# Gathered rows of the expert tiles moved inside SBUF on two DMA queues and transposed on VectorE, gates copied two tiles sooner

## The chip, the cores and the metric

The kernel runs on one core of one Trainium2 chip. The metric is the device time of one execution in microseconds (us); lower is better. The kernel before takes 640.49 us, the median of three runs (639.61 to 642.61).

A core has five engines with an instruction stream each, and they meet only through semaphores: TensorE (PE; its weight loads are listed as PEld), VectorE (DVE), ScalarE (ACT), GpSimd (POOL) and SyncE (SP), which here does nothing but issue DMAs. The 16 DMA engines of the core move the data. SBUF is the on-chip memory, PSUM the eight accumulator banks that TensorE writes.

## What is computed

The input is eight sequences of 512 tokens of width 256. After a layer norm, two branches are added to the residual: a causal linear attention with a second-order Taylor feature map (16 heads), and a mixture of eight experts in which each token goes to its top two.

```python
x  = L0_attn_hidden_states                      # (8, 512, 256) f32
xn = _layernorm(x)
x  = x + attention(xn, Wq, Wk, Wv, Wo) + experts(xn, Wg, W1, W2, W3)

# experts: E = 8, TOP_K = 2, DIM = 256, HID = 512
logits = xf @ Wg
top_w, top_i = top_k(logits, 2);  top_w = softmax(top_w)
h = einsum('nc,ech->enh', xf, W1)
g = einsum('nc,ech->enh', xf, W2)
y = einsum('enh,ehc->enc', silu(h) * g, W3)
out = einsum('enc,ne->nc', y, combine)          # combine holds top_w at the two experts
```

The kernel computes an expert only for the tokens that were sent to it: 8192 pairs of a token and an expert, sorted by expert in lists that are padded to whole tiles of 128 rows, 71 tiles in all (`NT`).

## The kernel before

**Attention first, experts after.** Up to about 300 us the kernel does the attention and the routing. On the way GpSimd scatters each normed token (256 values, 8 gates and its number) into a DRAM scratch, `xs_scr`, at its two places in the sorted lists. Then comes the loop over the 71 expert tiles, which this change is about.

**One expert tile t.** GpSimd gathers its 128 rows into a ring `xg` (`GR` = 4 slots, `gather`). TensorE transposes them in two halves into PSUM bank 4 (`transpose_g`, L1286). ScalarE copies the bank to `xgh` in a rounded format (L695), VectorE writes what the rounding left out to `xgl` (L1078), so that a product is made of three matmuls (high by high, high by low, low by high). Straight after that VectorE copies the gates and the row number from `xg` to a ring `xw` (L1083). TensorE computes h and g, six matmuls of 512 columns each (`up`, L1297). ScalarE applies silu to h (L722), VectorE multiplies by g into `hs` (L1112).

**The turn of s = silu(h) * g.** The second product needs s transposed. For tiles 8 to 68 (`TS` to `TE` - 1) this is not done by TensorE: SyncE issues four DMAs that regroup `hs` inside SBUF into `hq` (`move_h`, L450), two iterations later VectorE transposes `hq` in blocks of 32 x 32 into bank 5 (`turn_s`, L1088), ScalarE and VectorE split the bank into `sTh` (L706) and `sTl` (L1092), and TensorE runs the twelve matmuls of 256 columns (`down`, L1318) one iteration after. VectorE weighs the result with the gate (`weigh_y`, L1100) and GpSimd scatters it with an add into the output (`scatter`, L570).

**What sets the order.** Each engine's program is written out by hand as a loop over t; waits are semaphores counted. In iteration t from 11 on: TensorE does up(t, 0), up(t, 1), transpose_g(t+1), down(t-3). VectorE does the multiply of t, `xgl` and gates of t+1, turn_s(t-2), weigh_y(t-3), `sTl` of t-2. ScalarE does silu(t), `xgh` of t+1, `sTh` of t-2. SyncE does move_h(t), which waits for the multiply of t and, since `hq` has two slots, for turn_s(t-2). ScalarE's silu of t waits until move_h(t-2) has landed, since it writes into the slot of `hs` that this move reads. GpSimd issues gathers ahead of each scatter, up to t+7 ahead of scatter(t); a gather waits for the transposes and the copy of gates that last read its slot.

## Time and profile before

| | before |
|---|---|
| median of 3 runs | 640.49 us (639.61 to 642.61) |
| profiled execution, its own time | 641.93 us |
| profiled execution, span first to last instruction | 640.1 us |
| mean granted TensorE clock | 0.998 of full speed |
| PE busy in the span | 615.1 us (96%) |
| DVE, ACT, POOL busy | 450.3, 348.0, 360.3 us |
| bytes moved by DMA | 80.37 MB |

Busy time counts an engine's own instructions; issuing a DMA is not counted as busy. Matmuls overlap in the pipeline, so a matmul of 0.40 us can start 0.23 us after the one before it: what a matmul costs is the distance from start to start, not its duration. A wait is put down to whatever released it last. In the views by line, L numbers are lines of the kernel before.

### The profile page before, as it was taken

How to read it: one execution, taken by the hardware profiler on the slowest of the kernel's cores; microseconds unless marked ns; L12 is line 12 of the kernel's file. 1: busy time of each engine (PE TensorE's matmuls, PEld its weight loads, DVE VectorE, ACT ScalarE, POOL GpSimd, SP SyncE). 2: the span in 40 equal slices, each digit the busy share in tenths (PEclk: the TensorE clock that was granted, in tenths of full speed). 3: DMA queues.
4: the chain of work that ended last, by engine and by line, in shares of the span. 5: the costliest groups of instructions: out<-in, count | busy, mean ns of one | idle time of the engine just before them, and what ended most of it. 6: DMA issues, size and time to landing. Idle time of an engine off the chain costs nothing.

```text
span 640.1 us, 16670 instructions
## 1 busy us (share of the span) xinstructions
PE 615.1 (96%) x5181; PEld 475.5 (74%) x5181; DVE 450.3 (70%) x1134; ACT 348.0 (54%) x515; POOL 360.3 (56%) x453
## 2 busy tenths in 40 slices
PE   8899999999999999998899899999999999999995
PEld 8565665666666666655788788888888888888884
DVE  6876878787787776587787466666666667666663
ACT  3678878787878777775564233333333333333331
POOL 4265564737364654657167366566666666656645
PEclk9999999999999999999999999999999999999999
DMA  4753554545544444552953465656655656656553
GB/s 133 176 121 102 132 159 112 152 95 153 137 103 124 99 121 100 159 140 89 334 149 65 100 126 119 121 119 126 126 117 125 120 120 126 120 120 122 123 96 43
DMA packets 73347, 80.37 MB, mean 126 GB/s; under 512 B 12368, under 2 KB 61392, under 8 KB 73264
## 3 DMA queue, kind: packets, MB, share of 16 engines
q1 hardware_dynamic: 56144, 50.72, 30.1%
q0 software_dynamic: 16704, 28.12, 22.2%
q8 instruction: 48, 0.79, 0.5%
q10 hardware_dynamic: 416, 0.46, 0.3%
q14 instruction: 35, 0.29, 0.2%
HBM read 27.72 MB, written 22.95 MB: 79 GB/s over the span
## 4 chain that ended last, share of the span: by engine, by line
PE 43%; issue 26%; POOL 17%; DVE 8%; POOLq 2%; ACT 2%; DMA 0%; DVEq 0%; ACTq 0%
PE banks L1171 10%; POOL xg L544 9%; PE banks L1153 8%; PE banks L1191 7%; POOL out L570 6%; PE banks L1297 5%; PE banks L1200 4%; PE banks L1235 4%; POOL mark L556 3%; POOLq L554 2%; PE banks L1318 2%; PE banks L1220 2%; PE banks L1226 1%; ACT T L607 1%; DVE xTl L828 1%
## 5 line engine op out<-in xcount | busy, mean ns | idle before, releaser
L570 POOL DMA_INDIRECT out<-yo,xw x71 | 112.6, 1586 | 103.8 <-DVE yo L1100 99.9
L535 POOL TENSOR_SCALAR_AFFINE_SELECT T<-T 128x512 f32<-128x512 f32 x128 | 81.2, 646 | 108.6 <-ACT T L613 45.0
L1297 PE MATMUL banks<-w12h,xgh 128*128 x284 | 113.0, 398 | 3.4 <-DVE xgl L1078 3.3
L1297 PE MATMUL banks<-w12l,xgh 128*128 x284 | 111.4, 392 | 0.0
L1297 PE MATMUL banks<-w12h,xgl 128*128 x284 | 111.0, 391 | 0.0
L1112 DVE TENSOR_TENSOR hs<-banks,hs 128x512 f32<-128x512 f32 x71 | 49.1, 692 | 85.2 <-PE banks L1297 81.0
L706 ACT ACTIVATE sTh<-banks 128x512 fp32r<-128x512 f32 x71 | 42.4, 599 | 93.4 <-DVE banks L1088 76.8
L544 POOL DMA_INDIRECT xg<-xs_scr,glist x71 | 71.8, 1012 | 24.5 <-issue 19.7
L1171 PE MATMUL banks<-T,vau 128*17 128x512 f32 (+3 forms) x1024 | 75.5, 434 | 0.3 <-POOL T L535 0.3
L526 POOL DMA_INDIRECT xs_scr<-xb,slots x64 | 63.6, 994 | 19.0 <-issue 12.5
L1153 PE MATMUL banks<-Q,K 32*128 32x256 f32 (+2 forms) x1024 | 70.0, 358 | 2.0 <-DMA K<-Kt 1.8
L722 ACT ACTIVATE hs<-banks 128x512 f32<-128x512 f32 x71 | 42.4, 598 | 46.2 <-DMA hq<-hs 16.3
L599 ACT ACTIVATE T<-banks 128x1024 f32<-128x1024 f32 x64 | 62.1, 1027 | 10.0 <-PE banks L1153 9.4
L607 ACT ACTIVATE T<-banks 128x768 f32<-128x768 f32 x64 | 48.5, 810 | 29.1 <-PE banks L1153 26.4
L1297 PEld LDWEIGHTS banks<-w12h,xgh 128*128 128x128 f32 x284 | 53.6, 189 | 13.7 <-issue 4.8
L1297 PEld LDWEIGHTS banks<-w12h,xgl 128*128 128x128 f32 x284 | 53.3, 188 | 11.8
L695 ACT ACTIVATE xgh<-banks 128x256 fp32r<-128x256 f32 x71 | 27.3, 385 | 62.1 <-PE banks L1286 44.5
L1171 PEld LDWEIGHTS banks<-T,vau 128*17 128x17 f32 x1024 | 26.1, 97 | 45.5 <-issue 39.2
L1297 PEld LDWEIGHTS banks<-w12l,xgh 128*128 128x128 f32 x284 | 53.6, 189 | 8.1
L613 ACT ACTIVATE T<-banks 128x768 f32<-128x768 f32 x64 | 48.6, 809 | 19.0 <-PE banks L1153 18.5
L1092 DVE TENSOR_TENSOR sTl<-banks,sTh 128x512 fp32r<-128x512 f32 x71 | 48.9, 690 | 13.9 <-ACT sTh L706 11.1
L1153 PEld LDWEIGHTS banks<-Q,K 32*128 32x128 f32 x1024 | 38.4, 183 | 25.1 <-ACT T L599 10.9
(186 smaller groups left out, 1245.6 us busy)
## 6 DMA issues: line engine op xcount, KB each, us to landing
hq<-hs SPq DMA_DIRECT2D x244, 64.0 KB
w12r<-w SPq DMA_DIRECT2D x16, 512.0 KB, 4.4
Q<-Q SPq DMA_DIRECT2D x126, 64.0 KB, 2.4
out<-xa SPq DMA_DIRECT2D x16, 256.0 KB
w3r<-w SPq DMA_DIRECT2D x8, 512.0 KB, 7.1
K<-Kt SPq DMA_DIRECT2D x126, 32.0 KB
xa<-x SPq DMA_DIRECT2D x7, 512.0 KB, 4.8
xg<-xs_scr,glist POOLq DMA_INDIRECT x71
```

Source lines behind the costliest of these rows:

```text
L526: e.indirect_dma_start(xs_d, bass.IndirectOffsetOnAxis(slots[:, k, 4 * b + blk:4 * b + blk + 1].bitcast(U32), 0), xb[b % 2][:, blk, :], No ...
L535: e.affine_select(out=v, in_=v, pattern=[[0, 4], [1, P]], compare_op=ALU.is_ge, fill=-1.0, base=0, channel_multiplier=-1).then_inc(s["g_mk ...
L544: e.indirect_dma_start(xg[:, t % GR, :], None, xs_d, bass.IndirectOffsetOnAxis(glist[:, t:t + 1].bitcast(U32), 0)).then_inc(s[f"d_g{t % GR ...
L570: e.indirect_dma_start(out, bass.IndirectOffsetOnAxis(xw[:, t % XR, NE:NE + 1].bitcast(U32), 0), yo[:, t % 2, :], None, compute_op=ALU.add ...
L599: e.activation(T0[n % 2][:, 2 * h:2 * h + 2, :], banks[:, 2 * h:2 * h + 2, :], ACT.Square, scale=0.25, bias=1.0).then_inc(s["a_s"], 1)
L607: e.activation(T1[:, 2 * h:2 * h + 2, :], banks[:, 2 * h:2 * h + 2, 0:384], ACT.Square, scale=0.25, bias=1.0).then_inc(s["a_s"], 1)
L613: e.activation(T2[:, 2 * h:2 * h + 2, :], banks[:, 2 * h:2 * h + 2, P:512], ACT.Square, scale=0.25, bias=1.0).then_inc(s["a_s"], 1)
L1092: e.tensor_tensor(s_turned(sTl, t), s_bank(t), s_turned(sTh, t).bitcast(F32), ALU.subtract).then_inc(s["v_st"], 1)
L1112: e.tensor_tensor(h_turned(t), h_bank(t, 1), h_turned(t), ALU.mult).then_inc(s["v_mu"], 1)
L1153: i = e.matmul(banks[:, r, c0:c0 + w], K2[rr, g, h, jm * P:(jm + 1) * P], Q2[g][rr, h, p, 512 - w:512], start=(p == 0), stop=(p == 1))
L1171: i = e.matmul(banks[32 * r:32 * r + HA, 4, 512 - w:512], vau[b % 2][:, jm, 4 * qd + r, :], v[:, r, :], start=(jm == 0), stop=(jm == 2), s ...
L1297: i = e.matmul(banks[:, 2 * (t % 2) + m, :], a[:, k, :], w[:, bass.ds(expert[t] * 4 + (2 * k + m), 1), :], start=(k == 0 and n == 0), stop ...
```

## The change

The gathered rows of tiles 12 to 70 (`XS` = 12) take another way. Their two TensorE transposes are gone. Instead four DMAs regroup the gathered rows inside SBUF from `xg` into one of two buffers `xq` (`move_x`): quarters 0 and 1 of tile t+4 are issued by SyncE behind move_h(t), quarters 2 and 3 of tile t+3 by ScalarE behind its `xgh` copy. Each of the four moves 128 pieces of 64 values (256 bytes), where a move of `hs` has 128 pieces of 128 values. VectorE then transposes `xq` in blocks of 32 x 32 into bank 4 (`turn_x`, 128 x 256), and the copies to `xgh` and `xgl` read and write through strided views.

The rest follows from that or goes with it:
- The ring `xg` has three slots in place of four (its space holds an `xq` buffer), and the gathers are issued up to t+9 ahead of scatter(t), where it was t+7; for the first eight tiles t+4 where it was t+5.
- VectorE copies the gates of tile t+3 in iteration t, where it was t+1, into a ring of twelve (`XR`), where it was eight; nine values a row instead of sixteen.
- `up` waits for `xgh` alone before its first two matmuls, and for `xgl` only ahead of the third; before, it waited for `xgl` ahead of the first.
- The rows of W1 and W2 are laid out in pairs on the host, and the transposes of tiles 0 to 11 read every second column, so that both ways give the same order.

```diff
-GR = 4
+GR = 3
+XS = 12
-XR = 8
+XR = 12
+WI = NE + 1
@@
+        def move_x(e, t, some):
+            e.wait_ge(s[f"d_g{t % GR}"], 16 * (t // GR + 1))
+            if t >= XS + 2:
+                e.wait_ge(s["v_tx"], t - XS - 1)
+            for r in some:
+                e.dma_start(xq[t % 2][32 * r:32 * r + 32, :],
+                            xg[:, t % GR, 64 * r:64 * r + 64]).then_inc(s[f"d_xq{t % 2}"], 16)
+
+        def x_moved(e, t):
+            e.wait_ge(s[f"d_xq{t % 2}"], 64 * ((t - XS) // 2 + 1))
@@ SyncE
             for t in range(TS, TE):
                 move_h(t)
+                if XS <= t + 4 < NT:
+                    move_x(e, t + 4, range(2))
@@ GpSimd
                     e.wait_ge(s["v_xw"], t - GR + 1)
-                    e.wait_ge(s["p_gt"], t - GR + 1)
+                    if t - GR < XS:
+                        e.wait_ge(s["p_gt"], t - GR + 1)
+                    else:
+                        x_moved(e, t - GR)
@@
-                upto = t + 4 if t == 0 else t + 5 if t < TS else t + 7
+                upto = t + 3 if t == 0 else t + 4 if t < TS else t + 9
@@ ScalarE
             def expert_x(t):
-                e.wait_ge(s["p_gt"], t + 1)
+                if t < XS:
+                    e.wait_ge(s["p_gt"], t + 1)
+                else:
+                    e.wait_ge(s["v_tx"], t - XS + 1)
@@
                     expert_x(t + 1)
+                if XS <= t + 3 < NT:
+                    move_x(e, t + 3, range(2, 4))
@@ VectorE
+            def turn_x(t):
+                x_moved(e, t)
+                e.wait_ge(s["v_gt"], t)
+                e.transpose(banks[:, 4, 0:256], xq[t % 2].rearrange("p (t c k) -> p t k c", t=4, k=2)).then_inc(s["v_tx"], 1)
@@
                 if t + 1 < NT:
                     expert_x(t + 1)
+                if XS <= t + 2 < NT:
+                    turn_x(t + 2)
+                while weighed < min(t + 3 if t + 3 >= XS else t + 1, NT - 1):
+                    weighed += 1
+                    weights(weighed)
@@ TensorE
             def up(t, m):
-                e.wait_ge(s["v_gt"], t + 1)
+                e.wait_ge(s["a_gt"], t + 1)
...
+                        if k == 0 and n == 2:
+                            e.wait_ge(s["v_gt"], t + 1)
...
                 up(t, 1)
-                if t + 1 < NT:
+                if t + 1 < XS:
                     transpose_g(t + 1)
```

How the order moves is seen best on VectorE and SyncE. VectorE, one iteration late in the loop, before:

```order
L1112 TENSOR_TENSOR hs<-banks,hs 128x512 [waits p_g,a_si]
L1078 TENSOR_TENSOR xgl<-banks,xgh 128x256 [waits a_gt]
L1083 COPY xw<-xg 128x16 [waits d_sc1,d_g3]
L1088 STREAM_TRANSPOSE banks<-hq 128x512 [waits v_st,d_hq0]
L1095 TENSOR_LOAD texp
L1095 ISA x2
L1100 ISA [waits d_sc1,v_xw,p_yo]
L1100 TENSOR_SCALAR yo<-banks,xw 128x256
L1092 TENSOR_TENSOR sTl<-banks,sTh 128x512 [waits a_st]
```

And the same iteration now, where `xq_71` and `xq_72` are the two `xq` buffers:

```order
L1152 TENSOR_TENSOR hs<-banks,hs 128x512 [waits p_g,a_si]
L1110 TENSOR_TENSOR xgl<-banks,xgh 128x256 [waits a_gt]
L1115 STREAM_TRANSPOSE banks<-xq_72 128x256 [waits v_gt,d_xq1]
L1121 COPY xw<-xg 128x9 [waits d_sc0,d_g1]
L1126 STREAM_TRANSPOSE banks<-hq 128x512 [waits v_st,d_hq1]
L1133 TENSOR_LOAD texp
L1133 ISA x2
L1138 ISA [waits d_sc0,v_xw,p_yo]
L1138 TENSOR_SCALAR yo<-banks,xw 128x256
```

One transpose of 256 columns has come in ahead of the transpose of `hq`, and it waits for a DMA of its own. On SyncE's queue the loop before was move_h after move_h:

```order
L450 DMA hq<-hs 32x4x128 [waits v_th,v_mu]
L450 DMA hq<-hs 32x4x128 x3
L450 DMA hq<-hs 32x4x128 [waits v_th,v_mu]
L450 DMA hq<-hs 32x4x128 x3
```

Now two more issues stand between them; shown from where tile 8 begins:

```order
L472 DMA hq<-hs 32x4x128 [waits v_mu]
L472 DMA hq<-hs 32x4x128 x3
L354 DMA xq_71<-xg 32x4x64 [waits d_g0]
L354 DMA xq_71<-xg 32x4x64
L472 DMA hq<-hs 32x4x128 [waits v_mu]
L472 DMA hq<-hs 32x4x128 x3
L354 DMA xq_72<-xg 32x4x64 [waits d_g1]
L354 DMA xq_72<-xg 32x4x64
L472 DMA hq<-hs 32x4x128 [waits v_th,v_mu]
L472 DMA hq<-hs 32x4x128 x3
```

The move of `hs` of tile 9 stands behind a wait for the gather of tile 12 (`d_g0`). On ScalarE the two issues come between `xgh` and `sTh`:

```order
L725 ACTIVATE xgh<-banks 128x256 [waits p_g,v_tx]
L354 DMA xq_72<-xg 32x4x64 [waits v_tx,d_g2]
L354 DMA xq_72<-xg 32x4x64
L736 ACTIVATE sTh<-banks 128x512 [waits p_yo,v_th]
L752 ACTIVATE hs<-banks 128x512 [waits d_hq1,p_h]
```

The copy to `xgh` no longer waits for TensorE's transposes but for VectorE's (`v_tx`).

## Rows read from the trace of the kernel before

**Rows 1.** The page: busy us, share of the span and instructions of each engine.

```profile
PE 615.1 (96%) x5181; PEld 475.5 (74%) x5181; DVE 450.3 (70%) x1134; ACT 348.0 (54%) x515; POOL 360.3 (56%) x453
```

**Rows 2.** Busy time by stretch; columns as the first line says.

```profile
core 0: us, PE busy (x) PEld busy (x) DVE busy (x) ACT busy (x) POOL busy (x), PEclk, DMA share, GB/s
440.00:600.00 160.00, 159.77 (x946) 139.99 (x945) 106.25 (x220) 57.21 (x109) 101.22 (x109) 1.00 0.60 122
```

**Rows 3.** Timeline, TensorE: start us, us, engine, line, operation, tiles, count.

```profile
483.38 0.40 PE L1297 MATMUL banks<-w12h,xgl 128*128 x1
483.75 0.72 PE L1318 MATMUL banks<-w3h,sTh 128*128 x4
484.31 0.64 PE L1318 MATMUL banks<-w3l,sTh 128*128 x4
485.27 0.40 PE L1297 MATMUL banks<-w12h,xgh 128*128 x1
489.68 0.40 PE L1297 MATMUL banks<-w12h,xgh 128*128 x1
```

**Rows 4.** Timeline, VectorE, GpSimd and ScalarE in one tile.

```profile
483.88 0.69 DVE L1112 TENSOR_TENSOR hs<-banks,hs 128x512 f32<-128x512 f32 x1 [1.32 <-PE banks L1297]
488.29 0.69 DVE L1112 TENSOR_TENSOR hs<-banks,hs 128x512 f32<-128x512 f32 x1 [1.19 <-PE banks L1297]
488.42 1.00 POOL L544 DMA_INDIRECT xg<-xs_scr,glist  x1 [0.30 <-issue]
488.90 0.41 DVE L1078 TENSOR_TENSOR xgl<-banks,xgh 128x256 fp32r<-128x256 f32 x1
489.30 0.72 DVE L1088 STREAM_TRANSPOSE banks<-hq 128x512 f32<-128x512 f32 x1
490.06 0.48 DVE L1100 TENSOR_SCALAR yo<-banks,xw 128x256 f32<-128x256 f32 x1
490.82 1.59 POOL L570 DMA_INDIRECT out<-yo,xw  x1 [1.16 <-DVE yo L1100]
491.57 0.60 ACT L722 ACTIVATE hs<-banks 128x512 f32<-128x512 f32 x1 [0.92 <-DMA hq<-hs]
```

**Rows 5.** Timeline of SyncE's queue, four issues of one tile.

```profile
486.12 2.60 SPq L450 DMA_DIRECT2D hq<-hs  x4
```

**Rows 6.** Line 450, 430 to 610 us: duration ns min/median/max, first and last start.

```profile
L450 SPq DMA_DIRECT2D hq<-hs x163: 547/602/1887, 429.7 to 609.5; - x163
```

**Rows 7.** SyncE's waits, 420 to 600 us: us in total, times, longest us.

```profile
SPq L448 <- DVE banks L1088: 70.2, 40, 2.3
```

**Rows 8.** Waits of all engines, 420 to 600 us, same columns.

```profile
ACT hs L722 <- DMA hq<-hs: 10.0, 12, 1.9
```

**Rows 9.** Groups by line, 440 to 600 us: busy us, mean ns, idle before.

```profile
L706 ACT ACTIVATE sTh<-banks 128x512 fp32r<-128x512 f32 x36 | 21.5, 599 | 46.1 <-DVE banks L1088 46.1
L1286 PE MATMUL banks<-ident,xg 128*128 128x128 f32 x72 | 13.7, 271 | 0.0
```

**Rows 10.** DMA queues, 440 to 600 us: packets, MB, share of 16 engines.

```profile
q0 software_dynamic: 6964, 9.79, 37.5%
q1 hardware_dynamic: 20742, 9.45, 21.7%
```

**Rows 11.** TensorE's waits, 296 to 420 us.

```profile
PE banks L1297 <- DVE xgl L1078: 3.1, 5, 1.1
```

**Rows 12.** Timeline: the first gather and its use; gathers and waits near tile 10.

```profile
301.11 1.00 POOL L544 DMA_INDIRECT xg<-xs_scr,glist  x1 [0.15 <-issue]
303.99 0.20 PEld L1286 LDWEIGHTS banks<-ident,xg 128*128 128x128 f32 x2 [0.29 <-DMA xg<-xs_scr,glist]
...
355.95 1.01 POOL L544 DMA_INDIRECT xg<-xs_scr,glist  x1 [0.30 <-issue]
357.04 0.49 PE L1297 MATMUL banks<-w12h,xgh 128*128 x1 [1.06 <-DVE xgl L1078]
358.72 0.60 ACT L722 ACTIVATE hs<-banks 128x512 f32<-128x512 f32 x1 [2.32 <-DMA hq<-hs]
```

More of the change, by code:

```diff
@@ L178, in build @@
         xgl = rx.take("xgl", 256, F32R, (2, P))
-        xw = rx.take("xw", XR * 16, F32, (XR, 16))
+        xq = [rm.take("xq0", D), rx.take("xq1", D)]
+        xw = rx.take("xw", XR * WI, F32, (XR, WI))
         held = rx.take("held", 72, I32)
@@ L336, in s_turned, with x_bank, x_turned @@
             return v.rearrange("p (k c t) -> p k c t", k=4, t=4) if TS <= t < TE else v
+        def x_bank(t):
+            v = banks[:, 4, 0:256]
+            return v.rearrange("p (t k c) -> p k c t", t=4, k=2) if t >= XS else v.rearrange("p (k n) -> p k n", k=2)
+        def x_turned(tile, t):
+            return tile.rearrange("p k (c t) -> p k c t", t=4) if t >= XS else tile[:]
+        def move_x(e, t, some):
[7 more added lines that the diff above has]
+            e.wait_ge(s[f"d_xq{t % 2}"], 64 * ((t - XS) // 2 + 1))
         def x_landed(e, b):
@@ L691, in expert_x @@
             def expert_x(t):
-                e.wait_ge(s["p_gt"], t + 1)
+                if t < XS:
+                    e.wait_ge(s["p_gt"], t + 1)
+                else:
+                    e.wait_ge(s["v_tx"], t - XS + 1)
                 if t:
                     e.wait_ge(s["p_g"], t)
-                e.activation(xgh[:], banks[:, 4, 0:256].rearrange("p (k n) -> p k n", k=2), ACT.Copy).then_inc(s["a_gt"], 1)
+                e.activation(x_turned(xgh, t), x_bank(t), ACT.Copy).then_inc(s["a_gt"], 1)
             def high_s(t):
@@ L1077, in expert_x, with weights @@
                 e.wait_ge(s["a_gt"], t + 1)
-                e.tensor_tensor(xgl[:], banks[:, 4, 0:256].rearrange("p (k n) -> p k n", k=2), xgh[:].bitcast(F32),
-                                ALU.subtract).then_inc(s["v_gt"], 1)
+                e.tensor_tensor(x_turned(xgl, t), x_bank(t), x_turned(xgh, t).bitcast(F32), ALU.subtract).then_inc(s["v_gt"], 1)
+            def turn_x(t):
+                x_moved(e, t)
+                e.wait_ge(s["v_gt"], t)
+                e.transpose(banks[:, 4, 0:256], xq[t % 2].rearrange("p (t c k) -> p t k c", t=4, k=2)).then_inc(s["v_tx"], 1)
+            def weights(t):
                 e.wait_ge(s[f"d_g{t % GR}"], 16 * (t // GR + 1))
@@ L1284, in transpose_g @@
                     e.wait_ge(s["v_gt"], t)
+                pairs = xg[:, t % GR, 0:D].rearrange("p (n k) -> p k n", k=2)
                 for k in range(2):
-                    i = e.transpose(banks[:, 4, k * P:(k + 1) * P], xg[:, t % GR, k * P:(k + 1) * P], ident[:])
+                    i = e.transpose(banks[:, 4, k * P:(k + 1) * P], pairs[:, k, :], ident[:])
                 i.then_inc(s["p_gt"], 1)
@@ L1387 @@
         "wo": rows(wo),
-        "w12": w12.reshape(NE, 2, P, 2, HID).transpose(2, 0, 1, 3, 4).reshape(P, NE * 4, HID),
+        "w12": w12.reshape(NE, P, 2, 2, HID).transpose(1, 0, 2, 3, 4).reshape(P, NE * 4, HID),
         "w3": np.asarray(L0_ffn_W3).reshape(NE, 4, 4, 32, D).transpose(1, 3, 0, 2, 4).reshape(P, NE * 4, D),
```

7 lines of the change are left out of this document (5 added, 2 removed).

## The prediction, written before the changed kernel ran

> **What bounds the kernel now.** I read the busy times first. TensorE is busy for 615.1 of 640.1 us [rows 1], and from 440 to 600 us, deep in the expert tiles, for 159.77 of 160, at the full granted clock of 1.00 [rows 2]. There the reader is to see that nothing but TensorE is full: VectorE has 106.25 us of work in the 160, ScalarE 57.21, GpSimd 101.22. Next the timeline of one tile. The first matmul of a tile starts at 485.27 and that of the next at 489.68, so a tile takes 4.41 us [rows 3], and TensorE's instructions stand back to back in it. VectorE and ScalarE wait for TensorE: the multiply into `hs` sat idle for 1.19 us until the last `up` matmul [rows 4]. What is taken from TensorE is therefore won, as long as no loop between the others is longer than the new tile. So the views after that are the waits, for the loops that are nearly as long as a tile: ScalarE's silu waited for the move of `hs` to land in 12 of 41 tiles, 10.0 us in total [rows 8].
>
> **What TensorE loses.** The two transposes appear as 72 matmuls in 36 tiles [rows 9]; their 271 ns is pipelined and is not their price. The price is read from starts. From the last `up` matmul (483.38) over the transposes and the twelve `down` matmuls to the next tile's first (485.27) it is 1.89 us [rows 3]. Four `down` matmuls without a break take 0.48 us (485.27 less 484.31 is 0.96 for eight), so twelve take 1.44, and the step from an `up` matmul to the next instruction is 0.23. Without the transposes that makes 1.67, 0.22 us less. Tiles 12 to 70 lose them, 59 tiles: 59 x 0.22 = 13.0 us. The new tile is 4.19 us.
>
> **What the third matmul's wait gives.** TensorE waited for `xgl` five times at the head of a tile, 3.1 us in all, 1.1 at most [rows 11]; the one at 357.04 is at tile 10, where no `down` fills the time [rows 12]. Now only `xgh` is waited for, and the subtraction of 0.41 us [rows 4] lies beside two matmuls. Five times up to 0.4: between 0 and 2.0 us, I take 1.6.
>
> **What VectorE gets.** One transpose of 128 x 256 a tile. No such instruction is in the trace; the nearest are the 512-column transpose at 0.72 us and the 256-column subtraction at 0.41 [rows 4]. From 512 to 256 columns an elementwise pass falls by 0.69 - 0.41 = 0.28, so I take 0.44, with 0.41 and 0.72 as ends. VectorE's work goes from 106.25/160 x 4.41 = 2.93 us a tile to 3.37 of 4.19. It has room, but the new transpose stands ahead of the transpose of `hq`, so all that hangs on that one comes 0.4 us later against the multiply. The strided views of PSUM in the copies to `xgh` and `xgl` I cost at nothing: ScalarE's copy through such a view takes 599 ns [rows 9] and the silu of the same size through a plain one 0.60 us [rows 4]. The Trainium skill says, on "SBUF — State Buffer" (The DMA port swizzle), that PSUM has lines of 8 bytes and that a pattern that isn't contiguous slows matmuls by much. By that rule these copies would cost more; the trace does not agree for ScalarE's. The transposes of tiles 0 to 11 now read every second column: 24 instructions of 0.11 us. The ends are 0 and a doubling, 2.6 us; no row shows it, and I take 0, since the copies are indifferent to stride.
>
> **What ScalarE gets.** Two DMA issues a tile. SyncE's four take 2.60 us, 0.65 each [rows 5], with 547 to 1887 ns for one [rows 6]. ScalarE was idle for 46.1 us before 36 copies to `sTh`, 1.28 each [rows 9], which is just where the 1.3 us of issues fall, and these copies come 0.4 later anyway because of VectorE. Cost 0; without that cover up to the whole 1.3, but the `down` that reads `sTh` comes an iteration later.
>
> **What SyncE gets.** Two more issues, 1.3 us. It waited for the transpose of `hq` for 70.2 us in 40 tiles, 1.75 each [rows 7]. Less 0.22 of shorter tile and 1.3 of issues leaves 0.23 us a tile. This is the thinnest cover of all: at 0.69 us an issue it is gone.
>
> **The loop through `hq`.** Take the slow tile in the rows. Multiply at 483.88; issues from 486.12 to 488.72 [rows 5]; the silu that waited for their landing starts at 491.57, so landing took 2.8 us from the end of the issues; 0.60 of silu, 492.17; the multiply two tiles after the first comes at 483.88 + 8.82 = 492.70 [rows 4]. The loop takes 8.3 of 8.8 us. In 29 of 41 tiles the data had landed before the silu could start [rows 8], so the usual loop is shorter, I estimate 7.6. The change adds 0.4 (VectorE) and the room is now 8.38. The usual tile fits at 8.0; one like that in the rows (8.7) is late by 0.3 and eats into what lies between `xgl` and TensorE's need: the subtraction ended at 489.31, and `up` began at 489.68 [rows 3, 4] and now needs it two matmuls later. I charge 12/41 of 59 tiles, 17, with 0.07 us, 1.2 in all.
>
> **The DMA engines.** Their share is 0.60 [rows 2]. SyncE's queue used 21.7% of 16 engines for 20742 packets in 160 us, 26.8 ns a packet [rows 10]. The moves of x bring 512 packets of 256 bytes and 64 for semaphores a tile: 0.96 us a tile on all engines if each costs as much as a 512-byte one, 0.48 if by bytes. I take 0.7: the share goes to about 0.8. Against this, the scatter's time changes: the gather stands ahead of it and now waits for ScalarE's half of the move (issued 0.5 to 1.8 us after the multiply, landed some 2 later), so the scatter, which started 2.5 us after the multiply [rows 4], starts nearer to 5 us, and its writes no longer fall on the last move of `hs`. GpSimd can bear that: gather 1.00, scatter 1.59 and the small mark are 101.22/37 = 2.7 us of 4.19 a tile [rows 2, 4]. I let the two cancel. The Trainium skill, on "DMA: Bandwidth & Descriptors" (Specifications), wants at least 512 bytes a transfer, since below it the engine does a read-modify-write. No run here has shown packets of 256 bytes. By that rule they would cost at least the upper end, and with the last paragraph's loop it is the second rival below.
>
> **Where the new way begins.** SyncE issues quarters 0 and 1 of tile 12 ahead of the move of `hs` of tile 9 and waits for gather 12, which is issued behind scatter 7, at 355.95 [rows 12]. A gather was in use 2.9 us after it was issued (301.11 to 303.99), so SyncE is held until about 358.8 and begins the move of tile 9 near 360 instead of 356.6. The silu of tile 11 then waits for it some 2 us, of which TensorE's own backlog hides a part. Between 0 and 4 us, once; I take 1.5. The tighter ring of `xg` costs nothing elsewhere: a gather has more than two tiles from its issue to its first reader.
>
> **Sum.** The profiled execution takes 641.93 us, 1.83 outside its span. -13.0 - 1.6 + 1.2 + 1.5 = -11.9, so 630.0. That execution stands 1.44 above the median of the runs, 640.49, so the forecast is 628.6 us.
>
> **Rivals.**
> 1. *SyncE's queue becomes the bound.* If issues grow to 0.72 us beside ScalarE's, six and their two waits take 4.3 us or more, and the gain a tile falls from 0.22 to about 0.1: 59 x 0.1 = 6 us, 635. For it: 0.23 us of cover, single issues up to 1887 ns. Against: the median issue is 602 ns, the waits of SyncE are long in the mean.
> 2. *The loop through `hq` gets longer than two old tiles; slower than before.* Place: move of `hs`, landing, silu. If the packets of x share the engines with those of `hs` so that landing takes 0.9 us longer, the loop of a tile as in the rows is 8.3 + 0.4 + 0.9 = 9.6, a tile 4.8, and the end 59 x 0.39 = 23 later; with the usual tile, 7.6 + 0.4 + 0.9 = 8.9, it is 4.45 a tile and 59 x 0.04 = 2 later. Half of the tiles each: about 12 later, 653. It decides from 8.82 on, 0.8 more than the usual new loop. For it: 12 of 41 tiles wait already. Against: engines idle 0.4 of the time, and each wait that lengthens the tile gives the loop room.
> 3. *The tile is bound by landing of x.* SyncE's half is issued up to 6.2 us after the multiply and is wanted by `turn_x` at 2 x 4.19 + 1.0 = 9.4, so landing may take 3.2 us; in the slow tile that of `hs` took 2.8. If it takes 3.6, the tile is 4.4 long and nothing is won: 640.
>
> **Chances.** Forecast 0.58, with a range of its own of 625.5 to 632. Rival 1, 0.18. Rival 3 and other ways to a gain of nothing, 0.08. Rival 2, 0.13. Better than 625 (the waits for `xgl` and the move away from the scatter give more), 0.03. The range is 625.2 to 638.5: it leaves out rival 2, part of no change, and the best case. A change of under 0.5%, 3.2 us, can't be told from none: faster 0.77, same 0.09, slower 0.14.
>
> **What would show it.** Steady tiles of 4.19 us with TensorE back to back; the idle time of 1.06 before tile 10 down to about 0.6; a VectorE transpose of 128 x 256 at 0.44; SyncE's wait for the transpose of `hq` about 0.2 us a tile; ScalarE's silu waiting for the DMA more often than 12 in 41; the scatter later against the multiply; one loss of a microsecond or two at tiles 11 to 13. It is wrong if TensorE has gaps in steady tiles: ahead of `up` with `xgh` or `xgl` late, then it is the loop; or if SyncE never waits, then it is rival 1.

## The result and the profile after

Each kernel below is compared with runs of the kernel before on the same chip. One run of the changed kernel (649.47 us) counts as slow and is left out of the ratio.

| | before | after |
|---|---|---|
| median | 640.51 us (20 runs) | 643.96 us (20 runs, 639.67 to 649.47) |
| ratio, 95% interval | | 1.0046 (1.0033 to 1.0059) |
| profiled execution, its own time and span | 641.93, 640.1 | 644.40, 642.7 |

The changed kernel is 0.46% slower, with the whole interval above 1, but by less than the 0.5% that the prediction called no change; the forecast was 628.6 us, 1.9% faster. The runs also spread more widely than those of before. The busy times, as in [rows 1], and the stretch from 440 to 600 us, as in [rows 2]:

```profile
PE 610.5 (95%) x5063; PEld 465.3 (72%) x5063; DVE 471.1 (73%) x1193; ACT 343.8 (53%) x515; POOL 359.8 (56%) x453
```

```profile
440.00:600.00 160.00, 155.89 (x862) 132.12 (x860) 118.84 (x252) 54.43 (x109) 100.21 (x108) 1.00 0.74 151
```

TensorE was busy for 159.77 of the 160 us and now is for 155.89, though in a shorter tile it should have stayed full. VectorE is busy for 12.6 us more; its 36 new transposes of 0.46 us add up to 16.5, and in each kernel the records of neighbouring instructions overlap a little. The DMA share went from 0.60 to 0.74. The waits from 420 to 600 us (total us, times, longest), as in [rows 8] and [rows 7], first of all engines, then of SyncE's queue:

```profile
POOL xg L571 <- DMA xq<-xg: 46.7, 30, 4.0
ACT hs L752 <- DMA hq<-hs: 28.0, 28, 2.4
DVE hs L1152 <- ACT hs L752: 17.2, 19, 2.2
DVE yo L1138 <- DMA out<-yo,xw: 13.2, 18, 1.8
PE banks L1345 <- ACT xgh L725: 2.5, 4, 1.0
```

```profile
SPq L470 <- DVE banks L1126: 7.8, 13, 1.5
```

The silu waits for the move of `hs` in 28 tiles (12 before), and in 19 VectorE's multiply waits for the silu, which is not in the list of before. Next to it are two waits that did not exist: gathers wait for the moves of x, and VectorE's weighing for a scatter. SyncE waited 1.75 us a tile for the transpose of `hq`; now it waits in 13 tiles of some 40, for 7.8 us in all, 0.19 a tile.

One turn of the loop, one of the longer ones, in rows of VectorE, ScalarE and the two queues (a choice of rows; others stand between):

```profile
479.28 0.69 DVE L1152 TENSOR_TENSOR hs<-banks,hs 128x512 f32<-128x512 f32 x1 [0.40 <-ACT hs L752]
480.36 1.19 SPq L354 DMA_DIRECT2D xq<-xg  x2
481.65 2.48 SPq L472 DMA_DIRECT2D hq<-hs  x4
483.28 0.69 DVE L1152 TENSOR_TENSOR hs<-banks,hs 128x512 f32<-128x512 f32 x1 [0.39 <-ACT hs L752]
483.35 1.25 ACTq L354 DMA_DIRECT2D xq<-xg  x2
484.23 1.96 SPq L354 DMA_DIRECT2D xq<-xg  x2
486.28 2.49 SPq L472 DMA_DIRECT2D hq<-hs  x4
488.12 0.60 ACT L752 ACTIVATE hs<-banks 128x512 f32<-128x512 f32 x1 [1.95 <-DMA hq<-hs]
488.75 0.69 DVE L1152 TENSOR_TENSOR hs<-banks,hs 128x512 f32<-128x512 f32 x1 [0.31 <-ACT hs L752]
```

The multiply at 479.28 is followed two tiles later by that at 488.75: 9.47 us for two tiles, where two new tiles of 4.19 are 8.38. SyncE issues with pauses of about 0.1 us only, four, two, four. The four end at 484.13, and the silu that needs their data starts at 488.12, 4.0 us later; beside them run the other moves. That is a long landing, not the usual one: in the 28 tiles where the silu waited it started 2.87 us after the last of the four issues had ended, in the mean, and before, in 12 tiles, 3.01. The longest grew from 3.46 to 4.37 us. The next four start at 486.28 only, since the two of x before them took 1.96 us in place of 1.2, though the transpose they wait for had ended at 485.53:

```profile
484.82 0.71 DVE L1126 STREAM_TRANSPOSE banks<-hq 128x512 f32<-128x512 f32 x1
489.88 0.46 DVE L1115 STREAM_TRANSPOSE banks<-xq 128x256 f32<-128x256 f32 x1
```

The loop from a multiply to the one two tiles later can be added up from the traces (means of tiles 20 to 64; the landing from the tiles where the silu waited for it, so that the sums are those of such tiles):

| us, mean | before | after | e13, no moves of x |
|---|---|---|---|
| multiply | 0.69 | 0.69 | 0.69 |
| its end to the first issue of the move of `hs` | 1.16 | 1.98 | 1.64 |
| four issues | 2.60 | 2.69 | 2.57 |
| last issue's end to the silu | 3.01 | 2.87 | 2.85 |
| silu | 0.60 | 0.60 | 0.60 |
| sum | 8.06 | 8.83 | 8.35 |
| two tiles | 8.83 | 8.90 | 8.42 |

Before, the loop had 0.8 us of room; after, it has none to speak of. What grew is the time until SyncE begins the move. (e13, among the experiments below, keeps VectorE's new transpose and leaves out the moves.)

The DMA queues from 440 to 600 us, as in [rows 10], with ScalarE's q10 new:

```profile
q0 software_dynamic: 6900, 9.72, 37.9%
q1 hardware_dynamic: 31139, 11.83, 28.9%
q10 hardware_dynamic: 10368, 2.36, 7.0%
```

In what follows the *tile* is read from the rows of VectorE's multiply into `hs` between 400 and 605 us: count, durations, start of the first and of the last. Before, and after:

```profile
L1112 DVE TENSOR_TENSOR hs<-banks,hs x47: 690/692/694, 399.7 to 603.4; 128x512 f32<-128x512 f32 x47
```

```profile
L1152 DVE TENSOR_TENSOR hs<-banks,hs x46: 680/692/694, 400.3 to 600.5; 128x512 f32<-128x512 f32 x46
```

The first is 203.7 us over 46 steps, 4.43 us, the second 200.2 over 45, 4.45. So the tile that should have become 4.19 has not become shorter at all.

### The profile page after: what moved, and what is told of

The parts are those of the page before. It is cut to its first block, busy times and chain, and to the rows that moved or that the text cites. A ratio compares the mean times of both kernels' runs of the same rounds, so it can differ in the third digit from the quotient of the medians.

```text
span 642.7 us, 16840 instructions
## 1 busy us (share of the span) xinstructions
PE 610.5 (95%) x5063; PEld 465.3 (72%) x5063; DVE 471.1 (73%) x1193; ACT 343.8 (53%) x515; POOL 359.8 (56%) x453
## 3 DMA queue, kind: packets, MB, share of 16 engines
q10 hardware_dynamic: 17408, 4.33, 3.2%
## 4 chain that ended last, share of the span: by engine, by line
PE 54%; DMA 14%; DVE 10%; SPq 8%; issue 7%; ACT 3%; POOL 2%; POOLq 1%; DVEq 1%; ACTq 0%
PE banks L1345 11%; PE banks L1216 10%; DMA out<-yo,xw 8%; PE banks L1198 8%; PE banks L1236 7%; SPq L472 6%; PE banks L1366 5%; PE banks L1245 4%; PE banks L1280 3%; DMA hq<-hs 3%; DMA xq<-xg 2%; SPq L354 2%; PE banks L1265 2%; PE banks L1271 1%; PE banks L1306 1%
## 5 line engine op out<-in xcount | busy, mean ns | idle before, releaser
L1345 PE MATMUL banks<-w12h,xgh 128*128 x284 | 115.6, 407 | 8.9 <-ACT xgh L725 5.2
L1345 PE MATMUL banks<-w12h,xgl 128*128 x284 | 112.6, 396 | 0.0
L626 ACT ACTIVATE T<-banks 128x1024 f32<-128x1024 f32 x64 | 62.1, 1026 | 11.9 <-PE banks L1198 11.0
L1345 PEld LDWEIGHTS banks<-w12h,xgl 128*128 128x128 f32 x284 | 53.3, 188 | 16.3 <-DVE xgl L1110 4.2
L1216 PEld LDWEIGHTS banks<-T,vau 128*17 128x17 f32 x1024 | 26.1, 97 | 45.5 <-issue 40.7
L1138 DVE TENSOR_SCALAR yo<-banks,xw 128x256 f32<-128x256 f32 x71 | 34.0, 479 | 28.6 <-DMA out<-yo,xw 26.0
```

What stands on the lines that cost most here:

```text
L626: e.activation(T0[n % 2][:, 2 * h:2 * h + 2, :], banks[:, 2 * h:2 * h + 2, :], ACT.Square, scale=0.25, bias=1.0).then_inc(s["a_s"], 1)
L1216: i = e.matmul(banks[32 * r:32 * r + HA, 4, 512 - w:512], vau[b % 2][:, jm, 4 * qd + r, :], v[:, r, :], start=(jm == 0), stop=(jm == 2), s ...
L1345: i = e.matmul(banks[:, 2 * (t % 2) + m, :], a[:, k, :], w[:, bass.ds(expert[t] * 4 + (2 * k + m), 1), :], start=(k == 0 and n == 0), stop ...
```

## The experiments

The table has each ratio to the kernel before with its interval, and the tile; the single runs follow in the order in which they were made. Theory L blames VectorE's new transpose in the loop through `hq`, S the gather that waits for a move and holds the scatter, P the packets, Q the issues on the queues. e4, e5, e8, e9, e13, e14 and e15 leave data out, so that they measure time and compute wrong values; where they do, the counts that semaphores wait for are lowered to match, in lines that are not shown.

| run | what differs | ratio (interval) | tile, us |
|---|---|---|---|
| e1 | after, gathers to t+8 | 1.0069 (1.0039 to 1.0100) | 4.39 |
| e2 | after, new transpose last | 1.0060 (1.0033 to 1.0086) | 4.52 |
| e3 | both | 0.9962 (0.9937 to 0.9987) | 4.35 |
| e4 | before, no transposes | 0.9919 (0.9892 to 0.9947) | 4.30 |
| e5 | e4 with the later wait | 0.9787 (0.9755 to 0.9819) | 4.20 |
| e6 | before with the later wait | 0.9960 (0.9934 to 0.9985) | 4.40 |
| e7 | both, 1 issue SyncE, 3 ScalarE | 0.9967 (0.9941 to 0.9992) | 4.29 |
| e8 | both, no issues on SyncE | 0.9837 (0.9796 to 0.9877) | 4.20 |
| e9 | both, a quarter of the packets | 1.0069 (1.0035 to 1.0104) | 4.48 |
| e10 | both, every other tile moved | 0.9947 (0.9919 to 0.9976) | 4.38 |
| e11 | both, gathers to t+7 | 1.0018 (0.9991 to 1.0046) | 4.40 |
| e12 | every other tile, ScalarE alone | 1.1414 (1.1388 to 1.1440) | 5.77 |
| e13 | after without moves | 0.9851 (0.9820 to 0.9882) | 4.21 |
| e14 | after without new transposes | 0.9967 (0.9946 to 0.9988) | 4.36 |
| e15 | after without SyncE's half | 0.9971 (0.9947 to 0.9995) | 4.33 |
| e16 | e12, moves later | 0.9980 (0.9956 to 1.0003) | 4.31 |
| e18 | e16, gathers to t+7 | 0.9946 (0.9927 to 0.9965) | 4.28 |
| e19 | e18, moves from tile 16 on | 0.9905 (0.9881 to 0.9928) | 4.32 |

The tile comes from the one profiled execution of a kernel, the ratio from all its runs. The two can disagree: the profiled execution took 642.50 us in e1, where the median is 646.57, 651.19 in e2 (median 646.66) and 652.41 in e9 (median 649.44). How far a tile can be trusted is seen in e18 and e19: the same loop, and 4.28 and 4.32. A difference of less than about 0.04 is not read below.

**e1, e2, e3: two repairs of the order.** e1:

```diff
-                upto = t + 3 if t == 0 else t + 4 if t < TS else t + 9
+                upto = t + 3 if t == 0 else t + 4 if t < TS else t + 8
```

> The changed kernel with gathers issued up to t+8 ahead of scatter(t) in place of t+9, so that a gather no longer waits for a move of x that was only just issued. Theory S (the gather's wait holds the scatter back and VectorE's weighing waits for the scatter before): the wait of VectorE for the scatter, 13.2 us in 18 tiles from 420 to 600 us, goes to nearly nothing, and the time falls by 5 to 13 us, to about 631 to 638. Theory L (the loop through hq is too long, because VectorE's new transpose stands ahead of the old one and SyncE has two issues more): the scatter's wait goes but the time falls by less than 3 us, to 641 or more. Theory P (256-byte packets slow the landings): no change of the landings, less than 3 us.

e2 takes `turn_x(t + 2)` from behind `expert_x(t + 1)` and puts it last on VectorE:

```diff
                 if t - 2 >= TS:
                     low_s(t - 2)
+                if XS <= t + 2 < NT:
+                    turn_x(t + 2)
```

> The changed kernel with VectorE's new transpose of tile t+2 moved behind the low part of s of t-2, the last work of the iteration, so that the transpose of hq ends 0.45 us earlier against the multiply. Theory L: the loop loses 0.4 us of its 8.9, a tile 0.2, 59 tiles 8 to 12 us: 632 to 636. Theory S: the scatter still comes late, the gain is under 4 us, 640 or more. Theory P: under 4 us as well.

> Both edits. If S and L are both causes and neither alone suffices, this one falls to 628 to 632, the 4.19 us tile, and the two single edits to less than that. If P holds, landings stay at 2.5 us and above with single ones over 4, and the time stays above 636.

Neither edit alone gains: the ratios are 1.0069 and 1.0060. In e1 VectorE's wait for the scatter is gone from the list, as S said, and the time is not. In e2, where the gathers still ran nine tiles ahead, that wait was longer, 22.7 us against 13.2, in an execution of 651.19 us. Together they give 0.9962, less than a quarter of what was forecast. So neither L nor S is the sole cause, and yet each edit is worth something once the other is made: e1 and e3 differ in the place of the transpose alone, by 1.1%, and e2 and e3 in the gathers alone, by 1.0%. Behind both stands something else. In e3 SyncE's wait for the transpose of `hq` is

```profile
SPq L470 <- DVE banks L1126: 2.2, 3, 1.1
```

in 3 of 41 tiles. The view can miss waits; by the issues themselves, in 36 of 45 tiles (20 to 64) the transpose had ended before SyncE was done with the moves of x ahead of it. With the transpose 0.45 us earlier the queue was not ready for it, and that is theory Q, which came up only here. P, packets that slow the landings, had forecast more than 636 us for e3 as well, and 641.06 does not part the two; e9 does.

**e4, e5, e6: the gain by itself.** e4 and e5 leave out the two TensorE transposes of tiles 12 to 70; e5 and e6 have the change's wait in `up`.

```diff
-                if t + 1 < NT:
+                if t + 1 < 12:
                     transpose_g(t + 1)
```

```diff
             def up(t, m):
-                e.wait_ge(s["v_gt"], t + 1)
+                e.wait_ge(s["a_gt"], t + 1)
...
+                        if k == 0 and n == 2:
+                            e.wait_ge(s["v_gt"], t + 1)
```

> The kernel before without the two TensorE transposes of tiles 12 to 70 and nothing in their place: these tiles compute with the stale bank (the data is left out). It measures the term by itself. My sum: 59 x 0.22 = 13.0 us less, 627.5, with the loop through hq (8.3 us of now 8.4 in the slow tiles) eating up to 2 of it. If the loop binds even without the rest of the change, 631 or more.

> The kernel before without the TensorE transposes of tiles 12 to 70 (their data left stale) and with the later wait: up waits for xgh ahead of its first matmul and for xgl ahead of the third. In the run without transposes alone the steady tile was 4.30 us and the first up matmul had lost its prefetch of weights (0.33 to the second instead of 0.23). Theory X (there the tile was bound by the chain from the last up matmul over the multiply and xgl on VectorE): the tile falls to 4.19 to 4.21 and the time to 630 to 633. Theory L (the loop through hq binds as soon as the tile shrinks, even with nothing added): the tile stays at 4.25 to 4.30.

> The kernel before with the later wait for xgl alone. My term: 1.6 us less (0 to 2.0), from the five heads of tiles that waited; steady tiles stay at 4.41. Rival: nothing, within 0.5 us, since what the head wins the loop through hq takes back.

e4 gives 0.8%, 5 us, not 13. Its timeline points to the reason, rows of VectorE and TensorE:

```profile
485.15 0.69 DVE L1112 TENSOR_TENSOR hs<-banks,hs 128x512 f32<-128x512 f32 x1 [1.15 <-issue]
485.75 0.41 DVE L1078 TENSOR_TENSOR xgl<-banks,xgh 128x256 fp32r<-128x256 f32 x1
486.32 0.50 PE L1297 MATMUL banks<-w12h,xgh 128*128 x1
486.66 0.40 PE L1297 MATMUL banks<-w12l,xgh 128*128 x1
```

`xgl` is done at 486.16, `up` starts at 486.32, and its second matmul comes 0.34 us after its first, not 0.23. The second weight load started 0.24 us after the first matmul, where in the kernel before it starts together with it. I read that as a loop of 4.30 us through the end of `up`, the multiply, `xgl` and the next `up`, which the transposes had covered. With the later wait (e5) it is gone:

```profile
L1112 DVE TENSOR_TENSOR hs<-banks,hs x49: 691/692/693, 401.6 to 603.1; 128x512 f32<-128x512 f32 x49
```

201.5 us over 48 is 4.20, and the ratio 0.9787 of 643.75 us is 13.7 us less (11.7 to 15.8). So the loop through `hq` fits into tiles of 4.20 as long as nothing is added. e6 alone gives 0.9960, 2.6 us less (1.0 to 4.2).

**e7 to e11: issues, packets, gathers.** All are edits of e3. e7 leaves one quarter on SyncE and gives ScalarE two behind `xgh` and one behind `sTh`, with the gathers of e11:

```diff
-                    move_x(e, t + 4, range(2))
+                    move_x(e, t + 4, range(1))
...
-                    move_x(e, t + 3, range(2, 4))
+                    move_x(e, t + 3, range(1, 3))
...
+                    move_x(e, t + 3, range(3, 4))
```

e8 lets SyncE move x for tiles 12 and 13 only:

```diff
-                if XS <= t + 4 < NT:
+                if XS <= t + 4 < XS + 2:
                     move_x(e, t + 4, range(2))
```

e9 cuts each move from tile 14 on to a quarter:

```diff
+                n = 32 if t < XS + 2 else 8
-                e.dma_start(xq[t % 2][32 * r:32 * r + 32, :],
-                            xg[:, t % GR, 64 * r:64 * r + 64])
+                e.dma_start(xq[t % 2][32 * r:32 * r + n, :],
+                            xg[0:4 * n, t % GR, 64 * r:64 * r + 64])
```

e10 moves and turns only the even tiles:

```diff
+        def by_dma(t):
+            return XS <= t < NT and t % 2 == 0
...
-                if XS <= t + 4 < NT:
+                if by_dma(t + 4):
                     move_x(e, t + 4, range(2))
...
-                if t + 1 < XS:
+                if t + 1 < NT and not by_dma(t + 1):
                     transpose_g(t + 1)
```

e11 is e3 with the gathers one tile less ahead:

```diff
-                upto = t + 3 if t == 0 else t + 4 if t < TS else t + 8
+                upto = t + 3 if t == 0 else t + 4 if t < TS else t + 7
```

> The run with both edits (VectorE's new transpose last, gathers less far ahead), with gathers up to t+7 and the moves of x shared out as one quarter on SyncE and three on ScalarE (two behind xgh, one behind sTh). Theory Q (SyncE's queue is what binds: six issues and their waits fill 4.3 us of each tile, it waits for the transpose of hq in 3 of 41 tiles only): SyncE has 0.65 us room again, the tile falls from 4.34 to 4.20 to 4.25, time 631 to 635. Theory P (packets of x slow the landings): the packets are the same, the tile stays at 4.3 or above. Third: ScalarE's three issues delay sTh or silu, and the tile gets longer than 4.34.

> The run with both edits (gathers up to t+8), without SyncE's quarters of x from tile 14 on: half of the rows of x are left stale. SyncE is back at four issues a tile, ScalarE keeps its two, and half of the 256-byte packets remain. Theory Q: tile 4.19 to 4.23, time 629 to 633. Theory P: half of the effect of the packets is left, so half of the loss against 4.19: 4.26 or above, 635 or more.

> The run with both edits (gathers up to t+8, the new transpose last), with each move of x cut from tile 14 on to a quarter of its pieces, 32 of 256 bytes in place of 128 (three quarters of the rows of x are left stale). The number of issues on both queues stays. Theory Q (issues on SyncE's queue bind): tile as before at 4.32 to 4.35, the ratio to the kernel before within 0.3% of the one with both edits (0.996). Theory P (the packets on the shared engines bind, by longer landings and longer issues): tile 4.20 to 4.24, ratio 0.983 to 0.986, as in the run without SyncE's half, where issues and packets both went down.

> Both edits, and the way through SBUF for even tiles from 12 on only; odd tiles keep TensorE's transposes. SyncE has on average five issues a tile and ScalarE one. If the queues and the engines have room at this load, as in the run without SyncE's half, the tile is the mean of 4.41 and 4.20, 4.30 to 4.31, and with the later wait the ratio is 0.983 to 0.987, faster than both kernels. If the stalls come from single long issues and landings that any added move brings, it stays at 0.992 to 0.997.

> The run with both edits, with gathers only up to t+7 ahead of scatter(t) in place of t+8. There GpSimd still waited 17 us for moves of x and 22 us more ahead of gathers in 41 tiles. Theory S (what is left comes from the gather's wait): tile 4.34 to 4.25 or less. Theories Q and P: no change beyond 0.2%, since the scatter's landing is waited for by nobody any more.

e8 is the strongest of them. With SyncE back at four issues it was ready before the transpose in all of tiles 20 to 64, and the tile is 4.20, all that e5 has, though VectorE's transpose and ScalarE's half are in it:

```profile
L1152 DVE TENSOR_TENSOR hs<-banks,hs x49: 691/692/693, 401.5 to 603.2; 128x512 f32<-128x512 f32 x49
```

e8 also takes half of the packets away, so e9 keeps the issues and takes packets. It went the other way from what both theories said: slower than e3, 1.0069 against 0.9962. The issues of the small moves take longer than those of the whole ones (e9, then e3; min/median/max in ns):

```profile
L355 SPq DMA_DIRECT2D xq<-xg x91: 709/712/744, 399.4 to 602.8; - x91
```

```profile
L354 SPq DMA_DIRECT2D xq<-xg x94: 547/605/2152, 402.1 to 602.6; - x94
```

The DMA share of e9 fell to 0.63, from 0.78 in e3, and yet its tile is 4.48, longer than e3's 4.35. Added up over the trace, SyncE's six issues of a tile take 4.08 us in e9 and 3.88 in e3, 0.20 more, and the tile grew by 0.13. With the pauses between them (tiles 20 to 64) the queue of e9 is full: 2.83 us for the four, 0.10, 1.46 for the two, 0.14, in sum 4.53. The packets are not what binds. Nor did they get dearer where there were more of them: one of 512 bytes on SyncE's queue took 29.1 ns before, 29.3 after and 29.0 in e3.

e7 has all of e11's packets, one issue less on SyncE, and a tile of 4.29 against 4.40. That it isn't 4.20 leaves 0.09 us. This rest isn't SyncE's queue, which was ready before the transpose in 40 of 45 tiles; ScalarE's three issues or the packets remain, and no run parts these two. e7's whole time gained nothing over e3, since its start was slower: 19.6 us between the multiplies of tiles 8 and 12, 17.8 in e3.

e10 missed too: a tile of 4.38 in place of 4.30 to 4.31 and 0.9947 in place of 0.983 to 0.987, in the range that was given to stalls from any added move. SyncE was ready before the transpose in 41 of 45 tiles, so what is missing isn't its queue; it stays open. e11's expectation of no change failed as well: 1.0018 against 0.9962. The earlier scatter may fall on the last move of `hs` again; that is argued, not shown.

**e13, e14, e15: the change as it stands, less one part.** All three keep the change's order and its nine tiles of lead. e13 has moves for tiles 12 and 13 only:

```diff
-                if XS <= t + 4 < NT:
+                if XS <= t + 4 < XS + 2:
                     move_x(e, t + 4, range(2))
...
-                if XS <= t + 3 < NT:
+                if XS <= t + 3 < XS + 2:
                     move_x(e, t + 3, range(2, 4))
```

e14 has `turn_x` for these two only:

```diff
-                if XS <= t + 2 < NT:
+                if XS <= t + 2 < XS + 2:
                     turn_x(t + 2)
```

e15 is e8's edit on the change as it stands.

> The changed kernel without moves of x from tile 14 on (their data left stale); VectorE's new transpose stays where the change has it, ahead of the transpose of hq. Theory L (VectorE's 0.45 us in the loop through hq): tile 4.3 or above, ratio above 0.988. Theory Q (issues): the loop has room for 0.45 as soon as the queues are free, tile 4.20 to 4.22, ratio 0.977 to 0.982.

> The changed kernel with all moves of x and without VectorE's new transposes from tile 14 on (the bank is left stale; a move waits for the landing of the one two tiles before it, in place of the transpose). Theory L: the loop is 0.45 shorter, tile 4.25 or less, ratio 0.980 to 0.986. Theory Q: SyncE's six issues stay, tile 4.30 to 4.40, ratio 0.990 to 1.000.

> The changed kernel, order and gathers as they are, without SyncE's half of the moves from tile 14 on (half of the rows of x are left stale). Theory Q: tile 4.20 to 4.26, ratio 0.982 to 0.988, although the new transpose stands first. Theory L: with the order unchanged the tile stays at 4.35 or above, ratio 0.995 or above. Theory S (the gather waits for ScalarE's half, nine tiles ahead, and holds the scatter): this wait stays, so the tile stays above 4.35 too, with VectorE waiting for the scatter.

e13's rows, of the tile and of SyncE's wait:

```profile
L1152 DVE TENSOR_TENSOR hs<-banks,hs x48: 691/692/692, 403.2 to 601.1; 128x512 f32<-128x512 f32 x48
```

```profile
SPq L470 <- DVE banks L1126: 66.5, 42, 2.3
```

VectorE's transpose, even ahead of that of `hq`, costs nothing in the tile (4.21 against 4.20): the loop has room for the 0.46 as long as there are no moves, though only 0.07 us of two tiles is left, as the table of the loop shows. e13's ratio, 0.9851, missed its 0.977 to 0.982; from tile 8 to tile 12 it takes 18.1 us where e5 takes 16.3, which is about half of the difference, and the other half is open. L as the sole cause falls.

With the moves in, the transpose does cost: e14, all moves without it, has 0.9967 and 4.36 where the change has 1.0046 and 4.45, and e1 and e3 say the same. The moves without the transpose make the tile 0.16 longer than e5. Not all of that is SyncE's queue, though it had no break in 37 of 45 tiles; VectorE waited for scatters in 35 tiles, 41.6 us, since the gathers kept their nine tiles of lead.

ScalarE's half with the transpose (e15) makes it 4.33, and the ratio of 0.9971 is what L and S had forecast, not Q. SyncE waits there as in e13 (62.1 us in 36), but the gathers wait for ScalarE's half (45.5 us in 29) and VectorE for scatters in 9 tiles. In e8, with one tile less lead and the transpose last, the same half cost nothing. e8 and e15 differ in both, so no run says which of the two it is. The costs don't add. In the change's own order the tile goes from 4.21 to 4.33 with ScalarE's half and to 4.45 with SyncE's, and the whole time by 1.2% and then by 0.75% (e13, e15, the change). In e3's order it is nothing and then 0.15 us, or 1.25% (e8, e3).

**e10, e12, e16, e18, e19: a faster kernel.** Even tiles go by the moves, odd ones keep TensorE's transposes, the rest is as in e3. e10 shares the issues as the change does (ratio 0.9947). e12 puts all on ScalarE, and its waits for `sTh` follow:

```diff
-                if by_dma(t + 4):
-                    move_x(e, t + 4, range(2))
...
                     expert_x(t + 1)
+                if by_dma(t + 4):
+                    move_x(e, t + 4, range(2))
                 if by_dma(t + 3):
                     move_x(e, t + 3, range(2, 4))
```

> Even tiles from 12 on by the moves, odd ones by TensorE, as before, but with all four issues of a moved tile on ScalarE (two in each iteration) and none on SyncE. Theory Q: SyncE's queue is as it was, ScalarE's load is that of the run without SyncE's half, tile 4.30, ratio 0.984 to 0.988, the fastest full kernel. If it is the packets or the landings that cost, it equals the sharing of issues with SyncE: ratio 0.994 or above.

```profile
ACT sTh L743 <- issue: 80.5, 17, 5.4
```

731.54 us, where 0.984 to 0.988 of the kernel before was expected. ScalarE's queue stood behind a wait for gather t+4, whose slot TensorE frees only behind `up` of t, and `sTh` and the next silu stood behind it. e16 issues the moves an iteration later (two quarters of t+3 behind `xgh`, one behind `sTh`, the last behind the next silu), e18 has gathers to t+7, e19 begins at tile 16:

```diff
+                if by_dma(t + 2):
+                    move_x(e, t + 2, range(3, 4))
...
-                if by_dma(t + 4):
-                    move_x(e, t + 4, range(2))
                 if by_dma(t + 3):
-                    move_x(e, t + 3, range(2, 4))
+                    move_x(e, t + 3, range(2))
...
+                if by_dma(t + 3):
+                    move_x(e, t + 3, range(2, 3))
```

```diff
-XS = 12
+XS = 16
...
-                upto = t + 3 if t == 0 else t + 4 if t < TS else t + 8
+                upto = t + 3 if t == 0 else t + 4 if t < TS else t + 7
```

> Even tiles from 12 on by the moves, all on ScalarE and one iteration later than in the run that went to 731 us: two quarters behind xgh, one behind sTh, one behind the next silu, so that the gather has long landed. SyncE keeps its four issues. Theory Q: tile 4.30 to 4.33 (mean of 4.41 and 4.20, a little for ScalarE), ratio 0.984 to 0.990, faster than both kernels. If the cost lies in any added move, wherever it is issued, ratio 0.993 or above, as with one issue a tile on SyncE.

> Every other tile moved by ScalarE alone as in the run before, with gathers up to t+7 ahead of scatter(t) in place of t+8 (there GpSimd waited 41 us for TensorE's transposes ahead of gathers). Steady tile 4.30 to 4.31, tiles 8 to 12 in 17.5 us or less in place of 20.1, ratio 0.987 to 0.993. If the start costs by ScalarE's wait for gather 12 and not by the lead, it stays at 20 us and the ratio at 0.995 or above.

> The same with the moves from tile 16 on in place of 12, so that they begin when the gathers already run seven tiles ahead. Tiles 8 to 12 as with the later wait alone, 16.5 us, steady tile 4.30 to 4.31: ratio 0.986 to 0.990. If 0.993 or above, the remainder is not the start.

e16 had the steady tile that was expected and not the time (0.9980 for 0.984 to 0.990). Its start was slow: from the multiply of tile 8 to that of tile 12 it takes 20.1 us. e18's is 19.9, so the lead was not the cause of that; its ratio of 0.9946 missed the 0.987 to 0.993, and its tile of 4.28 is too near to 4.31 to be read as a gain. e19's start is 16.4. The multiplies of tiles 8 to 12, e16 and then e19:

```profile
L1163 DVE TENSOR_TENSOR hs<-banks,hs x5: 691/692/692, 353.2 to 373.3; 128x512 f32<-128x512 f32 x5
```

```profile
L1163 DVE TENSOR_TENSOR hs<-banks,hs x5: 691/692/692, 351.5 to 367.9; 128x512 f32<-128x512 f32 x5
```

e19 is the fastest complete kernel here: 634.81 us against 640.14, ratio 0.9905 (0.9881 to 0.9928), faster than before and after. Its expectation said 0.986 to 0.990; the tile is 4.32 where 4.30 was asked. About two fifths of the gain is the later wait, which alone gives 0.9960 (e6).

## Why the prediction was wrong

**TensorE's loss of the transposes, 13.0 us, and the later wait, 1.6.** Right as a sum: 14.6 forecast, 13.7 measured (e5). Wrong as two terms: the transposes alone are worth 5 us (e4), and the rest comes only with the later wait. I priced it by the five heads of tiles that waited before, and missed that it also unlocks the other term. The slack was in my rows: `xgl` ended at 489.31 and `up` began at 489.68, 0.37 us. In e4 0.16 us pass from one to the other when `up` waits, so 0.21 was left, against the 0.22 that I took away.

**VectorE's transpose.** Right in length, 0.46 us measured for 0.44, and without the moves it costs the tile nothing (e13). With them it does (e14, and e1 against e3), since the loop then has no room. The views through strides cost nothing that a trace shows: the copy to `xgh` takes 382 ns, before 385, and that to `xgl` 415, before 414.

**The start.** Right in size: 1.5 us forecast. From tile 8 to tile 12 the change takes 17.7 us and the later wait alone 16.5, 1.2 more (e13, e14 and e15, with the same start, take 18.0 to 18.3). Wrong in the place: ScalarE stands behind gather 12 too, and that was the nearer one. TensorE waits 1.56 us for `xgh` at tile 10:

```profile
358.50 1.48 ACTq L354 DMA_DIRECT2D xq<-xg  x2
360.09 0.60 ACT L752 ACTIVATE hs<-banks 128x512 f32<-128x512 f32 x1 [3.95 <-issue]
361.11 0.49 PE L1345 MATMUL banks<-w12h,xgh 128*128 x1 [1.56 <-ACT xgh L725]
```

**What failed: "I charge 12/41 of 59 tiles, 17, with 0.07 us, 1.2 in all", and with it the 0.23 us of cover for SyncE's queue and "I let the two cancel".** This is the term that was mis-sized, 1.2 us for what took the whole gain: (4.45 - 4.20) x 59 = 15 us. The same kernel without its moves has a ratio of 0.9851 (e13), with them 1.0046. I found room in each resource by itself, 0.23 us on SyncE, 0.4 in the loop, 0.2 of the DMA engines, and took the rooms as separate. They lie in one chain. SyncE's four issues wait for the transpose, the landing waits for the issues, the silu for the landing, the multiply for the silu, the next issues for the multiply. I let the loop grow by the transpose alone, 0.4 us. By the table of the loop it grew from 8.06 to 8.83: the first issue came 0.82 us later behind the multiply, where the transpose accounts for 0.46, and the rest comes with the moves of x (1.64 us in e13, 1.98 with them), since SyncE was still at work on those in 24 of 45 tiles.

SyncE's cover of 0.23 us was not there either. In the trace of after the four issues take 2.69 us and not 2.60, the two of x 1.30, and each of the two groups comes 0.10 us behind the one before at the least, where I had counted such a step once. That is 4.19 us, the whole of the tile that I forecast. The sign that I gave, SyncE waiting 0.2 us a tile, did come true (0.19), but in a tile of 4.45. A single issue of 1.9 us, which [rows 6] had at the same size before, fell into 1.75 us of idle time then and into 0.19 now. "Cost 0" for ScalarE's two issues failed as well: e15 has a tile of 4.33 where e13 has 4.21. By what way is open: by the gathers that wait for this half, or by the loop.

**The rivals.** Rival 1, SyncE's queue, at 0.18, is what binds in e3's order: e3, e8 and e9 agree on it. In the change's own order it is one of two parts, 0.12 us of the 0.24 a tile that the moves cost. Its price was too low, 635, since I took the length of an issue as what would have to grow. The median stayed at 602 ns and the mean at 0.64; the cover was missing from the start. Rival 2 was right about the place, the loop, and the silu's waits went from 12 to 28, but not about the cause or the size: the landing did not get 0.9 us longer but stayed at 2.9 for 3.0, and the tile is 0.02 us longer, within what can't be read, not 0.2. Rival 3's outcome, no gain, came true by another way. The gather's wait for ScalarE's half I had only used as a help against collisions, and had written that GpSimd can bear it. It can; VectorE's weighing, which needs the scatter two tiles on, waited for it in 18 tiles. What that costs by itself no run shows.

## What to carry to other kernels

Cover that lies in one chain counts once. Before adding issues to a queue, look for the loop that the queue is in, add up the loop and the queue for the new tile, the step from one group of issues to the next included, and compare the room that is left with the longer issues in the rows too. When work is taken from the bounding engine, ask which wait it was covering: here the transposes were worth 5 us alone and the later wait 2.6, and both together 13.7. A helper queue must not wait for a thing that the same tile frees; start a new scheme where its inputs already run ahead.

## What the runs showed of the hardware

The issue of a DMA cost the queue about 0.6 us for 128 pieces, of 512 bytes (median 602 ns, before) as of 256 (605, e3), and one that moves a quarter of the pieces cost more: 712 ns for 32 pieces of 256 bytes over 8 partitions (e9). The gathers and scatters cost GpSimd the same in all kernels, 0.99 and 1.59 us, while the DMA share ranged from 0.52 to 0.79.

A packet of 256 bytes cost less than one of 512, and more by the byte. Before, SyncE's queue carried 20742 packets and 9.45 MB in 21.7% of 16 engines over 160 us, 26.8 ns each [rows 10]; after, ScalarE's q10, with moves of x alone, carried 10368 packets and 2.36 MB in 7.0%, which is 17.3 ns each. Both counts hold packets of 4 bytes for semaphores. Without these, by size in the traces, it is 29.1 ns for 512 bytes and 18.3 for 256, 1.25 times as much by the byte. The 576 packets a tile of the prediction are 0.62 us on 16 engines at 17.3 ns, near the 0.7 that I took.

The Trainium skill, on "DMA: Bandwidth & Descriptors" (Specifications), says that transfers under 512 bytes miss line rate, since the engine reads, modifies and writes. The trace agrees as to the direction, 1.25 times the time for a byte, and not with the dearer packet that my second rival built on it.
